# Attention scores in rounded parts and rests, each head on half of the array's rows

## The chip, the cores and the metric

The kernel runs on one core of one Trainium2 chip. The metric is the device time of that core in microseconds (us), from the kernel's start to its end. TensorE (PE) multiplies; its weight loads are listed apart as PEld. VectorE (DVE) and ScalarE (ACT) read what PE leaves in the PSUM banks, GpSimd (POOL) and SyncE (SP) issue transfers. The engines run each their own list in order and wait for one another on semaphores.

## What is computed

A recommendation tower over 1024 rows. Two encoders give, for every row, four "states" of 512 real and 512 imaginary numbers. Attention with 8 heads of 64 follows over the four states of a row; the change is in its scores:

```python
qr = heads(sr @ Wq_r.T + bq_r)
qi = heads(si @ Wq_i.T + bq_i)
kr = heads(sr @ Wk_r.T + bk_r)
ki = heads(si @ Wk_i.T + bk_i)
ar = einsum('bhnd,bhmd->bhnm', qr, kr) + einsum('bhnd,bhmd->bhnm', qi, ki)
ai = einsum('bhnd,bhmd->bhnm', qi, kr) - einsum('bhnd,bhmd->bhnm', qr, ki)
mag = sqrt(ar ** 2 + ai ** 2 + 1e-08) * HD ** (-0.5)
w = softmax(mag)
out_r, out_i = w @ vr, w @ vi          # then @ Wo_r.T + bo_r, @ Wo_i.T + bo_i
```

After it come a mixing of the states by their phases, two measurement matrices, and three layers that end in one number per row.

## The kernel before, in words

Most matrix products are made in three passes of 32-bit "rounded" numbers (`split3`, lines 53 to 55): each operand is held as a rounded part (hi) and the rest (lo), and hi·hi, hi·lo and lo·hi are added up in a PSUM bank.

The change lies in `phase_states`, in its first half. It runs over 16 blocks `b` of 64 rows (256 columns, since each row has four states; `C` = 256). In a block, `m` = 0 to 3 counts slices of 128 of the 512 features, so that each slice holds two heads `h` of 64. PE's order in a block (`block_body` of the tensor engine) is written out by hand and sets the order of the rest:

- `project(b, m, 0)` makes the queries of slice m in bank `b_q` (one buffer), real part in one half of the columns and imaginary in the other; `project(b, m, 1)` the keys in `b_k[:, m % 2]` (two buffers). Each is 24 products of 256 columns.
- from m = 1 on, after both: `t_turn(b-1, m-1)` turns the softmax weights `pd` of the block before (4 transposes), `score(b, m-1)` makes the scores, and `mix(b-1, m-1)` multiplies the turned weights with the values.
- after m = 3: `values(b, 0)` and `(b, 1)`, then the turn, score and mix of slice 3, then `values(b, 2)` and `(b, 3)`, then `project_out(b-1, m)` for all four slices.

Before the change the queries leave `b_q` on ACT (`q_evac`, four reads of 64 partitions by 256, line 1287) into `qs`, and the keys leave `b_k` on DVE (`k_evac`, eight reads of 64 by 256, line 1590) into `ks`. Both are laid out so that real and imaginary parts of one head stand one above the other on the 128 partitions. `score` (line 2004) then needs one plain 32-bit product per head and column group: four per slice, each of 128 rows of the array and 256 columns; the profile lists each as two instructions. For a head and a group, the product gives the real and the imaginary score at once, into bank `b_sc[:, h]`.

On ACT a slice then goes `q_evac(b, m)`, `pt_evac(b-1, m-1)` (the turned weights, line 1302), `t_square(b, m-1)` (both score banks squared, line 1296), `o_high(b-1, m-1)` (rounded part of the mixed output, line 1311). On DVE it goes `spread(b-1, m)` (the weights `pd`, one buffer, so it waits for `t_turn(b-1, m-1)`; line 1639), `k_evac(b, m)`, `o_low(b-1, m-1)` (the rests of the output, line 1648), `pick(b, m-1)` (sum, mask and reduction of the squares, lines 1600 to 1609). At the end of a block `t_high` and `t_low` (lines 1339 and 1659) split the projected outputs into the buffer `at` (`thi`, `tlo`), and SP stores them (`store_a`).

Of the kernel before, what the change touches and what calls it, by code (L numbers as in the profile page):

```python
# [906 lines left out]
def phase_states(nc, g):  # L907
# [15 lines left out]
    with s.ctx:  # L923
# [11 lines left out]
        qs = sb_t("qs", [P, 2, 2, C])  # L935
        ks = sb_t("ks", [P, 2, 2, 2, C])
# [7 lines left out]
        at = sb_t("at", [P, 2, 2, 2, C], F32R)  # L944
        thi, tlo = at[:, 0], at[:, 1]
# [51 lines left out]
        k_read = [s.sem(f"t_k_read{h}") for h in range(2)]  # L997
# [88 lines left out]
        K_PARTS = ((0, 0, 0, 1), (0, 1, 1, 1), (1, 0, 1, 1), (1, 1, 0, -1))  # L1086
# [169 lines left out]
        @block.gpsimd  # L1256
        def _(pool):
            def fold(t):
                pool.wait_ge(folded, t * 2 + 1)
                if not isinstance(t, int) or t < LAST:  # L1260
                    pool.wait_ge(newton, t * 2 + 3)
                pool.wait_ge(stored, t * 16)
                pool.tensor_tensor(sup[:, :, :], cs[:, :, 2, :], cs[:, :, 3, :], ALU.add).then_inc(folded, 1)

            pool.memset(k01[:, 0:1], FLOOR).then_inc(k_made, 1)
            pool.memset(k01[:, 1:2], 1.0).then_inc(k_made, 1)
            pool.wait_ge(ids_in, 16)
# [12 lines left out]
        def _(act):  # L1280
            def q_evac(b, m):
                if not isinstance(b, int) or 4 * b + m >= 2:
                    act.wait_ge(scored, b * 8 + (2 * m - 2))
                act.wait_ge(projected, b * 8 + (2 * m + 1))
                for e in range(2):
                    for h in range(2):
                        ins = act.activation(qs[half(e), m % 2, h, :], b_q[half(h), e * C:(e + 1) * C], ACT.Identity,
                                             bias=bcol(M_Q + e, m, half(h)))
                    ins.then_inc(q_read, 1)
# [57 lines left out]
            def block_body(b, first):  # L1347
                q_evac(b, 0)
                for m in range(1, KD):
# [24 lines left out]

            blocks(act, block_body)
# [207 lines left out]
        def _(dve):  # L1583
            def k_evac(b, m):
                if not isinstance(b, int) or 4 * b + m >= 2:
                    dve.wait_ge(scored, b * 8 + (2 * m - 2))
                dve.wait_ge(projected, b * 8 + (2 * m + 2))
                for h in range(2):
                    for e, part, at_half, sign in K_PARTS:
                        ins = dve.tensor_scalar(ks[half(at_half), m % 2, h, part, :], b_k[half(h), m % 2, e * C:(e + 1) * C],  # L1590
                                                bcol(M_K + e, m, half(h)), float(sign), ALU.add, ALU.mult)
                    ins.then_inc(k_read[h], 1)
# [78 lines left out]
            def block_body(b, first):  # L1671
                k_evac(b, 0)
# [281 lines left out]
        def _(pe):  # L1954
            def project(b, m, i):

                pe.wait_ge(w_split, (M_Q, M_K)[i] * KD + 2 * KD)
                if i == 0:
                    if not isinstance(b, int) or 4 * b + m >= 1:
                        pe.wait_ge(q_read, b * 8 + 2 * m)  # L1960
                elif not isinstance(b, int) or 4 * b + m >= 2:
                    for h in range(2):
                        pe.wait_ge(k_read[h], b * 4 + (m - 1))
# [12 lines left out]
            def values(b, i):  # L1976
                pe.wait_ge(w_split, M_O * KD)
                e, gr = i // 2, i % 2
                if i == 2:
                    pe.wait_ge(q_read, b * 8 + 8)  # L1980
                elif i == 3:
                    for h in range(2):
                        pe.wait_ge(k_read[h], b * 4 + 3)
# [10 lines left out]
            def score(b, m):  # L1994
                pe.wait_ge(q_read, b * 8 + (2 * m + 2))
                for h in range(2):
                    pe.wait_ge(k_read[h], b * 4 + (m + 1))
                for h in range(2):
                    if not isinstance(b, int) or 4 * b + m >= 1:
                        pe.wait_ge(t_squared, b * 8 + (2 * m - 1 + h))  # L2000
                    for gr in range(NG):
                        cols = slice(gr * P, (gr + 1) * P)
                        out = b_sc[:, h, :].rearrange("p (a g c) -> p a g c", a=2, g=NG)[:, :, gr]
                        mm = pe.matmul(out, qs[:, m % 2, h, cols], ks[:, m % 2, h, :, cols], start=True, stop=True)
                    mm.then_inc(scored, 1)
# [222 lines left out]
def build(nc, g):  # L2228
    with ExitStack() as ctx:
# [12 lines left out]
        g.k01 = s.sb("k01", [P, 2])  # L2242
        s.align(512)
# [104 lines left out]
```

## Time and profile before

| what | value |
|---|---|
| median of three runs | 2947.16 us (2946.24 to 2949.06) |
| the profiled execution's own time | 2950.54 us |
| its span, first to last instruction | 2948.7 us |
| mean granted TensorE clock | 0.979 of full speed |
| PE busy | 2815.6 us, 95% of the span |
| PEld, DVE, ACT busy | 2438.5, 2105.5, 1326.6 us |
| the stage with the change | from about 1428 to 2330 us |

Busy time is summed over instructions of one engine; a matmul's duration in the profile includes the time in which its last columns run through the array, while the next one has already begun, so the pace of PE is read from the starts of its instructions in the timeline and not from their mean durations. A timeline row is: start, length, engine, line, operation, out<-in, shape, number of merged instructions, and in brackets how long the engine was idle before it and what ended that.

### The profile page before, as it was taken

The numbers are of one execution on the slowest core, as the hardware profiler recorded it, in microseconds if no ns is written. First come the engines' busy times: TensorE is split into PE (matmuls) and PEld (weight loads), VectorE is DVE, ScalarE is ACT, GpSimd is POOL, SyncE is SP. The second block draws the span as 40 slices with busy tenths as digits, with TensorE's granted clock in tenths as the row PEclk, the third lists the DMA queues.
The fourth block names the chain that finished last, engine by engine and source line by source line (L and its number), as shares of the span: only waits on it lengthen the run. The fifth ranks groups of instructions, "written<-read, shape, count | busy, mean of one in ns | idle before, by whom it ended". The sixth has DMA issues, their size and how long they took to land. (4 is left out here: it accounts for less than half of the span.)

```text
span 2948.7 us, 40983 instructions
## 1 busy us (share of the span) xinstructions
PE 2815.6 (95%) x15040; PEld 2438.5 (83%) x15040; DVE 2105.5 (71%) x3170; ACT 1326.6 (45%) x2000; POOL 139.8 (5%) x177
## 2 busy tenths in 40 slices
PE   8999999998999989999699999999999899999797
PEld 6888888886788877888599999999999877777686
DVE  5788768763668856787667667766776759999863
ACT  2222432243534344333455555555555654555553
POOL 1000100001001010000001001000000000000000
PEclk9999999998999999999899999999999999999899
DMA  6565465545738776486422232233223464344310
GB/s 241 188 208 187 170 225 189 187 138 179 244 113 263 251 254 202 142 266 242 172 58 58 79 92 57 59 91 78 57 71 94 105 163 103 93 101 123 111 40 11
DMA packets 493712, 420.36 MB, mean 143 GB/s; under 512 B 282272, under 2 KB 397088, under 8 KB 493344
## 3 DMA queue, kind: packets, MB, share of 16 engines
q1 hardware_dynamic: 459168, 341.20, 38.2%
q0 software_dynamic: 17792, 60.89, 5.4%
q10 hardware_dynamic: 16640, 16.78, 1.7%
q8 instruction: 70, 1.15, 0.2%
q14 instruction: 42, 0.34, 0.0%
HBM read 328.62 MB, written 90.18 MB: 142 GB/s over the span
## 5 line engine op out<-in xcount | busy, mean ns | idle before, releaser
L53 PE MATMUL banks<-a_hi 128*128 128x512 f32 x1024 | 399.6, 390 | 14.3 <-DVE a_lo L353 14.3
L54 PE MATMUL banks<-a_lo,a_hi 128*128 128x512 f32 x1024 | 399.3, 390 | 0.0
L55 PE MATMUL banks<-a_hi,a_lo 128*128 128x512 f32 x1024 | 399.3, 390 | 0.0
L53 PE MATMUL banks<-b_hi 128*128 128x512 f32 x896 | 357.0, 398 | 24.3 <-DVE b_lo L760 14.0
L55 PE MATMUL banks<-b_hi,b_lo 128*128 128x512 f32 x896 | 352.5, 393 | 0.0
L54 PE MATMUL banks<-b_lo,b_hi 128*128 128x512 f32 x896 | 352.4, 393 | 0.0
L53 PE MATMUL banks<-t_sx,g_hi 128*128 128x256 f32 x1024 | 294.6, 288 | 26.5 <-DMA t_sx<-s_scr 26.5
L54 PE MATMUL banks<-t_sx,g_hi 128*128 128x256 f32 x1024 | 291.5, 285 | 0.0
L55 PE MATMUL banks<-t_sx,g_lo 128*128 128x256 f32 x1024 | 291.5, 285 | 0.0
L1590 DVE TENSOR_SCALAR t_ks<-banks,cols 64x256 f32<-64x256 f32 x512 | 236.5, 482 | 75.2 <-PE banks L55 67.9
L53 PEld LDWEIGHTS banks<-a_hi 128*128 128x128 f32 x1024 | 192.9, 188 | 54.6 <-DVE a_lo L353 14.7
L55 PEld LDWEIGHTS banks<-a_hi,a_lo 128*128 128x128 f32 x1024 | 192.8, 188 | 40.2
L54 PEld LDWEIGHTS banks<-a_lo,a_hi 128*128 128x128 f32 x1024 | 192.8, 188 | 40.0
L53 PEld LDWEIGHTS banks<-b_hi 128*128 128x128 f32 x896 | 170.4, 190 | 66.0 <-DVE b_lo L760 28.8
L53 PE MATMUL banks<-g_hi,s_axng 128*128 128x512 f32 x512 | 203.6, 398 | 18.2 <-DVE s_cs L1732 14.6
L53 PEld LDWEIGHTS banks<-t_sx,g_hi 128*128 128x128 f32 x1024 | 198.4, 194 | 27.2 <-issue 23.1
L54 PE MATMUL banks<-g_lo,s_axng 128*128 128x512 f32 x512 | 202.5, 395 | 0.0
L55 PE MATMUL banks<-g_hi,s_axng 128*128 128x512 f32 x512 | 202.3, 395 | 0.0
L55 PEld LDWEIGHTS banks<-b_hi,b_lo 128*128 128x128 f32 x896 | 170.4, 190 | 36.4
L54 PEld LDWEIGHTS banks<-b_lo,b_hi 128*128 128x128 f32 x896 | 170.8, 191 | 34.3
L54 PEld LDWEIGHTS banks<-t_sx,g_hi 128*128 128x128 f32 x1024 | 198.5, 194 | 0.1
L55 PEld LDWEIGHTS banks<-t_sx,g_lo 128*128 128x128 f32 x1024 | 198.3, 194 | 0.0
(192 smaller groups left out, 5828.9 us busy)
## 6 DMA issues: line engine op xcount, KB each, us to landing
w_ring<-w_first SPq DMA_DIRECT2D x192, 512.0 KB, 4.3
w_ring<-w_second SPq DMA_DIRECT2D x160, 512.0 KB, 5.0
t_sx<-s_scr SPq DMA_DIRECT2D x64, 512.0 KB, 4.3
a_scr<-t_at SPq DMA_DIRECT2D x256, 128.0 KB, 1.9
s_axng<-a_scr SPq DMA_DIRECT2D x64, 512.0 KB, 5.4
g_wraw<-w_pieces SPq DMA_DIRECT2D x74, 256.0 KB, 4.7
x_raw<-h_scr ACTq DMA_DIRECT2D x16, 1024.0 KB, 7.0
w_ring<-w_second SPq DMA_DIRECT2D x64, 256.0 KB, 5.0
```

Of the source, the lines that this page charges most:

```text
L53: mm(out, ahi, bhi, start=first, stop=False, **more)
L54: mm(out, ahi, blo, start=False, stop=False, **more)
L55: return mm(out, alo, bhi, start=False, stop=last, **more)
L1590: ins = dve.tensor_scalar(ks[half(at_half), m % 2, h, part, :], b_k[half(h), m % 2, e * C:(e + 1) * C], bcol(M_K + e, m, half(h)), float(s ...
```

## The change

The scores are made in three passes of rounded parts and rests instead of one plain 32-bit product, and each head works on its own half of the array's rows. Real and imaginary parts are no longer stacked on the partitions: each is a separate product that is added up in the bank. So a slice has 2 column groups x 2 (real, imaginary) x 3 passes x 2 heads = 24 products of 64 rows and 256 columns, and heads alternate: head 0 reads partitions 0 to 63 and writes bank `b_sc[:, 0]`, head 1 partitions 64 to 127 and bank `b_sc[:, 1]`.

For that, queries leave `b_q` as whole reads of 128 partitions: ACT writes the rounded part (two reads), DVE then the rest (`q_rest`, two). The keys move from DVE to ACT for the rounded part (`k_evac` there, three reads: imaginary, real, negated imaginary), and DVE writes the rest (`k_rest`, three). `b_q` is free for the next `project(b, m+1, 0)` only when `q_rest` is done. `qs` takes over the buffer `at`, so `q_evac` of slices 0 and 1 waits for the stores of block b-2, and `t_square` of the slice before is waited for in both heads before the first score. A column of negated biases `nbk` is made once on POOL.

```diff
@@ scalar
             def q_evac(b, m):
                 if not isinstance(b, int) or 4 * b + m >= 2:
                     act.wait_ge(scored, b * 8 + (2 * m - 2))
+                if m < 2 and (not isinstance(b, int) or b >= 2):
+                    act.wait_ge(a_stored[m], b * 128 - 64)
                 act.wait_ge(projected, b * 8 + (2 * m + 1))
                 for e in range(2):
-                    for h in range(2):
-                        ins = act.activation(qs[half(e), m % 2, h, :], b_q[half(h), e * C:(e + 1) * C], ACT.Identity,
-                                             bias=bcol(M_Q + e, m, half(h)))
-                    ins.then_inc(q_read, 1)
+                    ins = act.activation(qs[:, 0, m % 2, e, :], b_q[:, e * C:(e + 1) * C], ACT.Identity, bias=bcol(M_Q + e, m))
+                ins.then_inc(q_high, 1)
+
+            def k_evac(b, m):
+                act.wait_ge(projected, b * 8 + (2 * m + 2))
+                bank = b_k[:, m % 2, :]
+                act.activation(ks[:, 0, m % 2, 0, :], bank[:, C:2 * C], ACT.Identity, bias=bcol(M_K + 1, m))
+                act.activation(ks[:, 0, m % 2, 1, :], bank[:, 0:C], ACT.Identity, bias=bcol(M_K, m))
+                act.activation(ks[:, 0, m % 2, 2, :], bank[:, C:2 * C], ACT.Identity, scale=-1.0,
+                               bias=g.nbk[:, m:m + 1]).then_inc(k_high, 1)
...
                     if not first:
                         pt_evac(b - 1, m - 1)
+                    k_evac(b, m)
                     t_square(b, m - 1)
@@ vector
-            def k_evac(b, m):
...
+            def q_rest(b, m):
+                dve.wait_ge(q_high, b * 4 + (m + 1))
+                for e in range(2):
+                    ins = dve.scalar_tensor_tensor(out=qs[:, 1, m % 2, e, :], in0=b_q[:, e * C:(e + 1) * C],
+                                                   scalar=bcol(M_Q + e, m), in1=f32(qs[:, 0, m % 2, e, :]),
+                                                   op0=ALU.add, op1=ALU.subtract)
+                ins.then_inc(q_read, 1)
+
+            def k_rest(b, m):
+                dve.wait_ge(k_high, b * 4 + (m + 1))
+                bank = b_k[:, m % 2, :]
+                for part, e in ((0, 1), (1, 0), (2, 1)):
+                    ins = dve.scalar_tensor_tensor(out=ks[:, 1, m % 2, part, :], in0=bank[:, e * C:(e + 1) * C],
+                                                   scalar=bcol(M_K + e, m), in1=f32(ks[:, 0, m % 2, part % 2, :]),
+                                                   op0=ALU.add, op1=ALU.subtract, reverse1=part == 2)
+                ins.then_inc(k_read, 1)
...
                     if not first:
                         spread(b - 1, m)
-                    k_evac(b, m)
+                    q_rest(b, m)
+                    k_rest(b, m)
                     if not first:
                         o_low(b - 1, m - 1)
                     pick(b, m - 1)
@@ tensor
             def score(b, m):
...
+                q, k = qs[:, :, m % 2], ks[:, :, m % 2]
+                passes = [(e, x, y) for e in range(2) for x, y in ((0, 0), (0, 1), (1, 0))]
+                for gr in range(NG):
+                    cols = slice(gr * P, (gr + 1) * P)
+                    for i, (e, x, y) in enumerate(passes):
+                        for h in range(2):
+                            bank = b_sc[:, h, :].rearrange("p (a g c) -> p a g c", a=2, g=NG)[:, :, gr]
+                            mm = pe.matmul(bank, q[half(h), x, e, cols], k[half(h), y, 1 - e:3 - e, cols],
+                                           start=i == 0, stop=i == len(passes) - 1)
+                            if gr == NG - 1 and i == len(passes) - 1:
+                                mm.then_inc(scored, 1)
```

PE's list before, between the projections of slice 3 and the values (line 2014 is `t_turn`, 2004 `score`, 2025 `mix`; an `x4` stands for four products in a row):

```order
L55 MATMUL banks<-t_sx,g_lo 128x256
L2014 MATMUL banks<-ident,t_pd 128x128 x4
L2004 MATMUL banks<-t_ks,t_qs 128x2x128 x4
L2025 MATMUL banks<-t_ptl,t_v 128x128 x4
L53 MATMUL banks<-g_hi,t_sx 128x512
```

The same place after (`score` is line 2026 there):

```order
L55 MATMUL banks<-t_sx,g_lo 128x256
L2038 MATMUL banks<-ident,t_pd 128x128 x4
L2026 MATMUL banks<-t_ks,t_qs 128x2x128 x24
L2049 MATMUL banks<-t_ptl,t_v 128x128 x4
L53 MATMUL banks<-g_hi,t_sx 128x512
```

Nothing moves on PE; four products become 24.

DVE's list before, in the loop over the blocks, from slice 1's `spread` to that of slice 2 (`t_ks` is the keys' reads, `t_olo` the output's rests, `t_m` and `t_mg` the picking; the rows of registers belong to waits):

```order
L1639 SCALAR_TENSOR_TENSOR t_pd<-t_ex,t_inv,mask 128x128 x4
L1587 REGISTER_ALU
L1590 TENSOR_SCALAR t_ks<-banks,cols 64x256 x8
L1645 ISA
L1648 SCALAR_TENSOR_TENSOR t_olo<-banks,cols,t_ohi 64x256 x4
L1598 REGISTER_ALU
L1600 TENSOR_TENSOR t_m<-t_sq 128x512
L1604 REGISTER_ALU
L1605 TENSOR_TENSOR t_m<-t_m,mask 128x512
L1609 TENSOR_REDUCE t_mg<-t_m 128x16
L1637 REGISTER_ALU
L1639 SCALAR_TENSOR_TENSOR t_pd<-t_ex,t_inv,mask 128x128 x4
```

The same stretch after:

```order
L1659 SCALAR_TENSOR_TENSOR t_pd<-t_ex,t_inv,mask 128x128 x4
L1598 REGISTER_ALU
L1600 SCALAR_TENSOR_TENSOR t_qs<-banks,cols,t_qs 128x256 x2
L1609 SCALAR_TENSOR_TENSOR t_ks<-banks,cols,t_ks 128x256 x3
L1665 ISA
L1668 SCALAR_TENSOR_TENSOR t_olo<-banks,cols,t_ohi 64x256 x4
L1616 ISA
L1620 TENSOR_TENSOR t_m<-t_sq 128x512
L1625 TENSOR_TENSOR t_m<-t_m,mask 128x512
L1629 TENSOR_REDUCE t_mg<-t_m 128x16
L1657 REGISTER_ALU
L1659 SCALAR_TENSOR_TENSOR t_pd<-t_ex,t_inv,mask 128x128 x4
```

Eight reads become five, and the queries' rests now stand behind `spread`.

ACT's list before, the stretch of slice 2 in the loop:

```order
L1287 ACTIVATE t_qs<-banks,cols 64x256 x4
L1299 REGISTER_ALU
L1302 ACTIVATE t_ptl<-banks 128x512
L1295 REGISTER_ALU
L1296 ACTIVATE t_sq<-banks 128x512
L1293 REGISTER_ALU
L1296 ACTIVATE t_sq<-banks 128x512
L1311 ACTIVATE t_ohi<-banks,cols 64x256 x4
```

The same after:

```order
L1290 ACTIVATE t_qs<-banks,cols 128x256 x2
L1309 REGISTER_ALU
L1312 ACTIVATE t_ptl<-banks 128x512
L1294 REGISTER_ALU
L1296 ACTIVATE t_ks<-banks,cols 128x256
L1297 ACTIVATE t_ks<-banks,cols 128x256
L1298 ACTIVATE t_ks<-banks,g_nbk 128x256
L1305 REGISTER_ALU
L1306 ACTIVATE t_sq<-banks 128x512 x2
L1321 ACTIVATE t_ohi<-banks,cols 64x256 x4
```

The keys' three reads now stand between the turned weights and the squares.

## Rows read from the trace of the kernel before

**Rows 1.** The page: PE's busy time; granted clock in 40 slices of the span.

```profile
PE 2815.6 (95%) x15040; PEld 2438.5 (83%) x15040; DVE 2105.5 (71%) x3170; ACT 1326.6 (45%) x2000; POOL 139.8 (5%) x177
...
PEclk9999999998999999999899999999999999999899
```

**Rows 2.** Busy time by stretches; the attention stage.

```profile
core 0: us, PE busy (x) PEld busy (x) DVE busy (x) ACT busy (x) POOL busy (x), PEclk, DMA share, GB/s
...
1425.00:2330.00 905.00, 901.18 (x6435) 855.75 (x6435) 635.96 (x1485) 485.08 (x939) 30.85 (x32) 1.00 0.27 75
```

**Rows 3.** Groups by form, 1425 to 2330 us: busy, mean ns | idle before.

```profile
L1590 DVE TENSOR_SCALAR t_ks<-banks,cols 64x256 f32<-64x256 f32 x512 | 236.5, 482 | 75.2 <-PE banks L55 67.9
...
L2004 PE MATMUL banks<-t_ks,t_qs 128*128 128x256 f32 x512 | 121.2, 379 | 0.0
...
L1648 DVE SCALAR_TENSOR_TENSOR t_olo<-banks,cols,t_ohi 64x256 fp32r<-64x256 f32 x240 | 115.9, 483 | 6.5
...
L1339 ACT ACTIVATE t_at<-banks,cols 128x256 fp32r<-128x256 f32 x112 | 47.0, 471 | 79.2 <-DMA a_scr<-t_at 63.9 <-PE banks L55 15.2
```

**Rows 4.** Timeline of PE, slice 1 of a block, to the next turn.

```profile
1599.70 0.60 PE L2014 MATMUL banks<-ident,t_pd 128*128 128x128 f32 x4
1600.13 1.89 PE L2004 MATMUL banks<-t_ks,t_qs 128*128 128x256 f32 x8
1601.86 1.05 PE L2025 MATMUL banks<-t_ptl,t_v 128*128 128x128 f32 x8
1602.67 0.36 PE L53 MATMUL banks<-t_sx,g_hi 128*128 128x256 f32 x1
...
1604.91 0.28 PE L53 MATMUL banks<-t_sx,g_hi 128*128 128x256 f32 x1
1605.27 0.28 PE L53 MATMUL banks<-t_sx,g_hi 128*128 128x256 f32 x1
...
1608.51 0.60 PE L2014 MATMUL banks<-ident,t_pd 128*128 128x128 f32 x4
```

**Rows 5.** Timeline of DVE, the same stretch.

```profile
1600.34 1.14 DVE L1639 SCALAR_TENSOR_TENSOR t_pd<-t_ex,t_inv,mask 128x128 f32<-128x128 f32 x4 [2.41 <-PE banks L2014]
1601.51 3.79 DVE L1590 TENSOR_SCALAR t_ks<-banks,cols 64x256 f32<-64x256 f32 x8
1605.33 1.99 DVE L1648 SCALAR_TENSOR_TENSOR t_olo<-banks,cols,t_ohi 64x256 fp32r<-64x256 f32 x4
1607.35 0.69 DVE L1600 TENSOR_TENSOR t_m<-t_sq 128x512 f32<-128x512 f32 x1
...
1609.41 1.13 DVE L1639 SCALAR_TENSOR_TENSOR t_pd<-t_ex,t_inv,mask 128x128 f32<-128x128 f32 x4
```

**Rows 6.** Timeline of ACT, the same stretch.

```profile
1600.41 0.60 ACT L1302 ACTIVATE t_ptl<-banks 128x512 f32<-128x512 f32 x1 [1.46 <-PE banks L2014]
...
1602.06 0.60 ACT L1296 ACTIVATE t_sq<-banks 128x512 f32<-128x512 f32 x1 [0.18 <-PE banks L2004]
1602.96 1.93 ACT L1311 ACTIVATE t_ohi<-banks,cols 64x256 fp32r<-64x256 f32 x4 [0.29 <-PE banks L2025]
```

**Rows 7.** Weight loads of the turns: group over the stage, and one slice's timeline.

```profile
L2014 PEld LDWEIGHTS banks<-ident,t_pd 128*128 128x128 f32 x240 | 28.2, 140 | 2.0
...
1608.41 0.46 PEld L2014 LDWEIGHTS banks<-ident,t_pd 128*128 128x128 f32 x4
```

**Rows 8.** Timelines of DVE, ACT and PE at a block's end and the next's beginning.

```profile
1638.51 1.13 DVE L1659 SCALAR_TENSOR_TENSOR t_at<-banks,cols,t_at 128x128 fp32r<-128x128 f32 x4 [1.13 <-ACT t_at L1339]
...
1644.35 1.13 DVE L1659 SCALAR_TENSOR_TENSOR t_at<-banks,cols,t_at 128x128 fp32r<-128x128 f32 x4 [1.62 <-ACT t_at L1339]
...
1643.41 0.84 ACT L1339 ACTIVATE t_at<-banks,cols 128x256 fp32r<-128x256 f32 x2 [2.21 <-DMA a_scr<-t_at]
...
1649.00 1.93 ACT L1287 ACTIVATE t_qs<-banks,cols 64x256 f32<-64x256 f32 x4 [1.60 <-PE banks L55]
...
1648.80 0.28 PE L53 MATMUL banks<-t_sx,g_hi 128*128 128x256 f32 x1
```

More of the change, by code:

```diff
@@ L943, in phase_states @@
         olo = sb_t("olo", [P, KD, 2, C], F32R)
-        at = sb_t("at", [P, 2, 2, 2, C], F32R)
-        thi, tlo = at[:, 0], at[:, 1]
+        qs = sb_t("qs", [P, 2, 2, 2, C], F32R)
+        thi, tlo = qs[:, 0], qs[:, 1]
         mg2 = sb_t("mg2", [P, KD, GH, N])
@@ L996, in phase_states @@
         q_read = s.sem("t_q_read")
-        k_read = [s.sem(f"t_k_read{h}") for h in range(2)]
+        k_read = s.sem("t_k_read")
+        q_high = s.sem("t_q_high")
+        k_high = s.sem("t_k_high")
         v_full = s.sem("t_v_full")
@@ L1266, in _ @@
             pool.memset(k01[:, 1:2], 1.0).then_inc(k_made, 1)
+            pool.tensor_scalar(g.nbk[:, :], g.cols[:, COL_BC + (M_K + 1) * KD:COL_BC + (M_K + 2) * KD], -1.0, None,
+                               ALU.mult).then_inc(k_made, 1)
             pool.wait_ge(ids_in, 16)
@@ L1348, in block_body @@
                 q_evac(b, 0)
+                k_evac(b, 0)
                 for m in range(1, KD):
@@ L1373, in block_body @@
                         t_high(b - 1, m)
+            act.wait_ge(k_made, 3)
             blocks(act, block_body)
@@ L1583, in _ @@
         def _(dve):
-            def k_evac(b, m):
[L1585 to L1592, printed above, removed]
+            def q_rest(b, m):
[13 more added lines that the diff above has]
+                ins.then_inc(k_read, 1)
             def pick(b, m):
@@ L1671, in block_body @@
             def block_body(b, first):
-                k_evac(b, 0)
+                q_rest(b, 0)
+                k_rest(b, 0)
                 for m in range(1, KD):
@@ L1959, in project @@
                     if not isinstance(b, int) or 4 * b + m >= 1:
-                        pe.wait_ge(q_read, b * 8 + 2 * m)
+                        pe.wait_ge(q_read, b * 4 + m)
                 elif not isinstance(b, int) or 4 * b + m >= 2:
-                    for h in range(2):
-                        pe.wait_ge(k_read[h], b * 4 + (m - 1))
+                    pe.wait_ge(k_read, b * 4 + (m - 1))
                 if m == 0 and not (isinstance(b, int) and b == 0):
@@ L1979, in values @@
                 if i == 2:
-                    pe.wait_ge(q_read, b * 8 + 8)
+                    pe.wait_ge(q_read, b * 4 + 4)
                 elif i == 3:
-                    for h in range(2):
-                        pe.wait_ge(k_read[h], b * 4 + 3)
+                    pe.wait_ge(k_read, b * 4 + 3)
                 elif not isinstance(b, int) or b >= 2:
@@ L1994, in score @@
             def score(b, m):
[L1995 to L2005, printed above, removed]
+                pe.wait_ge(q_read, b * 4 + (m + 1))
+                pe.wait_ge(k_read, b * 4 + (m + 1))
+                if not isinstance(b, int) or 4 * b + m >= 1:
+                    pe.wait_ge(t_squared, b * 8 + 2 * m)
+                q, k = qs[:, :, m % 2], ks[:, :, m % 2]
[9 more added lines that the diff above has]
+                                mm.then_inc(scored, 1)
             def t_turn(b, m):
@@ L2242, in build @@
         g.k01 = s.sb("k01", [P, 2])
+        g.nbk = s.sb("nbk", [P, KD])
         s.align(512)
```

4 lines of the change are left out of this document (1 added, 3 removed).

## The prediction

> **What bounds the kernel now.** I read the page first: PE is busy for 95% of the span, at a granted clock of 0.8 to 1.0 [rows 1]. Then the busy times by stretches: in the stage that the change touches PE is busy for 901.2 of 905.0 us at full clock, DVE for 636.0 and ACT for 485.1 [rows 2]. So in this stage the time is PE's list of work, and a change is worth what it adds to or takes from that list, unless it makes PE wait. Then the timeline of one slice, counted from T, the start of its turn (1599.70): turn 0.43 us, score 1.73, mix 0.81, then two projections of 24 products each up to the next turn at T+8.81 [rows 4]. In the projections three products start every 0.36 us, so one every 0.12 us [rows 4]; nowhere does PE pause. DVE is a close second: its round of spreading, reading keys, output rests and picking takes from 1600.34 to 1609.41, 9.07 us, more than PE's 8.81 [rows 5]. It may fall behind for three slices since the keys have two banks and the time is made good while PE makes the values. ACT has room.
>
> **PE's part of the change.** Away go 8 instructions per slice, which take 1.73 us [rows 4]; their mean length of 379 ns [rows 3] holds the run through the array and isn't the pace. In come 24 products of 64 rows and 256 columns in rounded numbers. A product of that kind with 128 rows is paced at 0.12 us [rows 4]. The trace shows no product on half of the rows, so I bound the score time S from both sides:
> - heads fully side by side, 12 pairs by 0.12: S = 1.44 us. A still lower floor takes the spacing of the turns' weight loads, four in 0.46 us where one has 0.14, so (0.46 - 0.14) / 3 = 0.107, times 12: S = 1.28 [rows 7].
> - heads one after the other: 24 by 0.12, S = 2.88.
> - a price for going over to half arrays and back: a product is listed with 0.28 us but the next starts after 0.12 [rows 4], so 0.16 us of running through is hidden today. If PE has to run empty at both changes, that and one load of 0.11 are paid twice: 0.54 us per score. With pairs, S = 1.98; in series, S = 3.42.
>
> I take pairs, with half of the price of changing over: S = 1.44 + 0.27 = 1.71, nearly what it is today. The nearest fact in the rows is that loads and products of different instructions already go on together: PE and PEld are busy for 95% and 83% of the same span [rows 1]. The profile has nothing that speaks for or against the price, which is why I take its middle.
>
> What the Trainium skill says of it, in "TensorEngine Tiling (Array Packing)", Key Properties: different tiles of the array can load weights and multiply in parallel, but changing the tiling mode drains TensorE. By that page S would be 1.98 and the sum below about 9 us higher; no row of the trace shows either half of the rule.
>
> **The other engines' part.** DVE loses 8 reads of 482 ns and gains 5 of the kind that takes 483 [rows 3]: the rows' number of partitions doesn't count, their 256 elements do. That is 3.79 us against 5 x 0.483 = 2.42 per slice, 88 us less over 64 slices. ACT loses 4 reads of 0.48 (1.93 for the output's four of this shape, [rows 6]) and gains 5 of 0.471 (a 128x256 read, [rows 3]): 0.43 us more per slice. Neither is on the path by its sum. But the order matters, so I walk slice 1 of a block, in times from T:
>
> - ACT: turned weights at 0.71 to 1.31 [rows 6]. Then the keys' three rounded reads, 3 x 0.483 = 1.45: to 2.78 (they are projected before T). Then two squares of 0.60, which before started as soon as a bank was scored (the second at 2.36, [rows 6]) and now queue: to 4.02. Then the output's four rounded reads, 1.93: to 5.97 instead of 5.19 (1602.96 + 1.93).
> - DVE: spreading starts at 0.64 [rows 5], takes 1.17 with its gap, then the queries' rests 0.97 to 2.78, the keys' rests from 2.83 to 4.28. It then waits for ACT: 5.97 plus 0.10 (the step from ACT to DVE, 1643.41 + 0.84 to 1644.35, [rows 8]) = 6.07. Output rests 2.0 to 8.08, picking as before 2.06 until the next spreading can start (1607.35 to 1609.41, [rows 5]): 10.15.
> - Slice 2: DVE spreads 10.15 to 11.32, queries' rests to 12.28. Only now is `b_q` free. PE, which waits with `project(b, 3, 0)` behind mix, starts its first product after a step of 0.05 and a weight load of 0.11: T+12.43.
> - Before, that product came at one slice and the 2.97 us from turn to projection (1602.67 - 1599.70, [rows 4]): T+11.78. So the block loses 0.65 us here, whatever S is, as long as S stays below 2.0 or so: with S at 1.71, PE is there at T+8.79+2.95 = 11.74 and stands idle for 0.7.
>
> In slice 1 the rests are ready at T+2.83 and wanted at 0.43 + S + 0.81 = 2.95: nothing. In slice 3 no projection follows, and the picking of slice 2 ends in time. So per block with a block before it the sum is 0.65 + 2 x (S - 1.73), where the factor 2 is for the scores of slices 2 and 3, made after the wait; with S = 1.71 it is 0.61 us. Fifteen blocks: 9.2 us. Block 0 has no turn and no mix, and gets 4 x (S - 1.73) = -0.1. Sum +9.1 us.
>
> **What is hidden.** The queries share their buffer with outputs. The store of slice 0's output takes 3.77 us from the end of its split (1638.51 + 1.13) to the ACT read that it lets go (1643.41) [rows 8]. Slice 2's split ends at 1645.48, so its buffer is free at 1649.25; the queries' first read stood at 1649.00 [rows 8] and slips by 0.25. With 0.95 for it, 0.15 for two steps and 0.97 for the rests, `b_q` is free at 1651.32; PE wants it after the keys' 24 products, 1648.80 + 2.88 = 1651.68. The projection of the keys hides it, by 0.36 us; were a store later than that, it would cost what it is later, 14 times. SP and POOL get no new work in the loop; the negated bias column is one small POOL instruction. Waiting for both squares ahead of a score costs nothing: they end at 4.0, the next score starts at 9.2. The later last reads at the end of the stage lie beside the output projections.
>
> **Rivals.**
> 1. Weights are loaded in series though products run side by side. Then the 24 loads pace the score, 24 x 0.107 = 2.57 us [rows 7]: 0.84 more per slice, PE no longer waits for DVE, 64 x 0.84 = 53.8 us, 3001.0 us. For it: the turns' loads come 0.107 us apart although their products have half as many columns as the projections' [rows 7], as if the loads set that pace. Against it: loads of different halves read different partitions. The Trainium skill, "TensorE: Matmul & The Clock Gate", LDWEIGHTS, says that a load's time goes by its columns and not by its rows, so half of the rows saves nothing; it also says there, in Part 3, that a load overlaps running products only where the row groups differ, which the busy shares contradict: 95% and 83% of one span overlap, and all of it at 128 rows [rows 1].
> 2. The heads don't run side by side at all, the change doesn't do what it says: S = 2.88, 64 x 1.15 = +73.6, 3020.8 us; with the price of changing over, 64 x 1.69 = +108, 3055. For it: each row of PE in this trace has the form 128*128, so side-by-side work isn't seen once.
> 3. The other side, faster: pairs at 1.44, and PE never waits for `b_q`. That is decided on ACT: the output's rounded reads would have to end by about T+4.8 instead of 5.97, so that DVE spreads for slice 2 at T+9.0. Then each of the 64 scores gives 0.29 us: -18.6, 2928.6 us. For it: DVE has 88 us less work, and its order has slack that I may have walked too strictly. Against it: the same walk, made for the kernel before, gives 9.71 for DVE's next spreading, and it is at 1609.41 - 1599.70 = 9.71.
>
> **How the numbers follow.** The profiled execution took 2950.54 us, its span 2948.7; by the sum it would take 2959.6. The median of the runs lies 3.4 lower, at 2947.16, and the forecast goes by it: 2947.16 + 9.1 = 2956.3. The forecast's own range is that of S with pairs: S = 1.28 gives 15 x (0.65 - 0.90) - 1.8 = -5.6, 2941.6; S = 1.98 gives 15 x 1.15 + 1.0 = +18.3, 2965.4.
>
> Chances: forecast 0.50; rival 1, 0.19; rival 2, 0.19; rival 3, 0.12. The range 2938 to 3024 leaves out most of rival 3 and the costly end of rival 2. A measurement here can tell 0.2%, 5.9 us, from no change. Faster by more than that is rival 3 alone, 0.12. Within it lies the forecast with S below about 1.6, 0.22. Slower: the rest of the forecast, 0.28, and rivals 1 and 2, 0.66 in all.
>
> **What would show it.** In the timeline of PE after: the score of a slice, from its first product's start to the mix's, is S; two products of a pair start together if heads run side by side, and loads too. A wait of some 0.7 us ahead of the first projection of slice 3, ended by the queries' rests on DVE, and none ahead of slice 2's, shows the walk right; ACT's output reads should start near T+4.0. DVE's busy time should fall by 88 us, ACT's rise by some 27. The prediction is wrong if S is over 2.0, or if PE shows no wait, or if stores end later than the keys' projection hides.

## The result

The changed kernel takes 2955.06 us (median of 7 runs, 2951.81 to 2960.46), the kernel before 2947.74 (7 runs, 2946.17 to 2950.52). The ratio is 1.0026, with an interval from 1.0015 to 1.0038: 7.3 us slower. The forecast was 2956.3, slower by 9.1.

The page of the changed kernel, its busy times and granted clock:

```profile
PE 2824.7 (95%) x16064; PEld 2440.5 (82%) x16064; DVE 2003.2 (68%) x2978; ACT 1319.7 (45%) x2064; POOL 142.4 (5%) x178
...
PEclk9999999999999999999899999999999999999899
```

Against [rows 1] DVE has 102 us less and PE 9 more. ACT was forecast with 27 more and has 7 less.

The profiled execution's span is 2958.7 us, 10.0 more than before. Not all of that is the change. The same kernel, profiled again further below, has a span of 2949.2; the stretch from the last values of the stage to the end, which the change doesn't touch, takes 2958.7 - 2335.7 = 623.0 us in one and 2949.2 - 2333.2 = 616.0 in the other (622.1 before). So the stage itself must be compared: from its first product on PE, at 1424.3 us, to the last that the values begin with a `L53`, it takes 2335.7 - 1424.3 = 911.4 us (2333.2 - 1423.3 = 909.9 in the second profile) against 2326.6 - 1423.7 = 902.9 before. The change is worth 7.0 to 8.5 us there, as in the medians. These are the rows of the values' products, of the kernel before and then of the changed one. Each gives the shortest, median and longest duration in ns, and then the first and last start:

```profile
L53 PE MATMUL banks<-g_hi,t_sx x256: 389/389/580, 1454.3 to 2326.6; 128*128 128x512 f32 x128
```

```profile
L53 PE MATMUL banks<-g_hi,t_sx x256: 388/390/500, 1456.4 to 2335.7; 128*128 128x512 f32 x128
```

The same slice as in [rows 4 to 6], the first of its block that has a turn (slice 1 in the prediction's count), now on PE, weight loads, DVE and ACT (T = 1603.88 is the start of the turn):

```profile
1603.88 0.60 PE L2038 MATMUL banks<-ident,t_pd 128*128 128x128 f32 x4
1604.41 1.69 PE L2026 MATMUL banks<-t_ks,t_qs 64*128 64x256 f32 x24
1606.03 1.16 PE L2049 MATMUL banks<-t_ptl,t_v 128*128 128x128 f32 x8
1606.95 0.36 PE L53 MATMUL banks<-t_sx,g_hi 128*128 128x256 f32 x1
...
1612.78 0.60 PE L2038 MATMUL banks<-ident,t_pd 128*128 128x128 f32 x4
```

```profile
1604.41 1.49 PEld L2026 LDWEIGHTS banks<-t_ks,t_qs 64*128 64x128 f32 x24 [0.17 <-issue]
```

```profile
1604.52 1.14 DVE L1659 SCALAR_TENSOR_TENSOR t_pd<-t_ex,t_inv,mask 128x128 f32<-128x128 f32 x4 [3.69 <-PE banks L2038]
1605.58 0.87 DVE L1600 SCALAR_TENSOR_TENSOR t_qs<-banks,cols,t_qs 128x256 fp32r<-128x256 f32 x2
1606.36 1.26 DVE L1609 SCALAR_TENSOR_TENSOR t_ks<-banks,cols,t_ks 128x256 fp32r<-128x256 f32 x3
1609.19 1.99 DVE L1668 SCALAR_TENSOR_TENSOR t_olo<-banks,cols,t_ohi 64x256 fp32r<-64x256 f32 x4 [1.56 <-ACT t_ohi L1321]
```

```profile
1604.60 0.60 ACT L1312 ACTIVATE t_ptl<-banks 128x512 f32<-128x512 f32 x1 [2.55 <-PE banks L2038]
1605.09 0.47 ACT L1296 ACTIVATE t_ks<-banks,cols 128x256 fp32r<-128x256 f32 x1
1605.45 0.48 ACT L1297 ACTIVATE t_ks<-banks,cols 128x256 fp32r<-128x256 f32 x1
1605.80 0.48 ACT L1298 ACTIVATE t_ks<-banks,g_nbk 128x256 fp32r<-128x256 f32 x1
1606.22 1.09 ACT L1306 ACTIVATE t_sq<-banks 128x512 f32<-128x512 f32 x2
1607.23 1.92 ACT L1321 ACTIVATE t_ohi<-banks,cols 64x256 fp32r<-64x256 f32 x4
```

PE first. The array form now reads 64*128. The 24 products start within 1.69 - 0.28 = 1.41 us, 0.061 apart, 0.12 a pair: the heads do run side by side, and so do their loads, 24 in 1.49 us. But the score's own gain is eaten at its edges. From turn to score it is 0.53 us (before 0.43), from score to mix 1.62 (1.73), from mix to the first projection 0.92 (0.81): 3.07 in all instead of 2.97. A slice takes 8.90 us instead of 8.81.

On DVE and ACT: the keys' rounded reads are listed with 0.47 each but start 0.36 apart; three of DVE's end within 1.26 us. And PE doesn't wait for the rests outside block 0 and the last block. All of PE's waits in the stage that the waits view lists:

```profile
PE banks L53 <- DMA t_sx<-s_scr: 4.0, 1, 4.0
...
PE banks L53 <- DVE g_lo L1688: 1.4, 1, 1.4
...
PE banks L53 <- issue: 0.5, 1, 0.5
```

The first was 3.8 us before. The second is new and comes once, in block 0:

```profile
1445.79 1.69 PE L2026 MATMUL banks<-t_ks,t_qs 64*128 64x256 f32 x24
1448.92 0.36 PE L53 MATMUL banks<-t_sx,g_hi 128*128 128x256 f32 x1 [1.44 <-DVE g_lo L1688]
```

On DVE eight weight pieces (`g_lo`) stand ahead of the queries' rests that PE waits for; the view names the pieces, and the rests end at 1448.82:

```profile
1443.13 4.90 DVE L1688 TENSOR_TENSOR g_lo<-g_wraw,g_hi 128x512 fp32r<-128x512 f32 x8
1447.95 0.87 DVE L1600 SCALAR_TENSOR_TENSOR t_qs<-banks,cols,t_qs 128x256 fp32r<-128x256 f32 x2
```

One more wait is too short for that list. It is the wait of the prediction's walk, ahead of the first projection of slice 3, and it comes in the last block alone:

```profile
2312.32 0.88 DVE L1600 SCALAR_TENSOR_TENSOR t_qs<-banks,cols,t_qs 128x256 fp32r<-128x256 f32 x2
```

```profile
2313.29 0.36 PE L53 MATMUL banks<-t_sx,g_hi 128*128 128x256 f32 x1
```

The projection starts 0.09 us behind the end of the rests and 1.09 behind the first product of mix, instead of 0.92: PE loses 0.17 us, in both profiles of the kernel. DVE began its spreading there 1.09 us after the turn, and elsewhere 0.64 to 0.71 after it. In the other blocks the rests of this slice end 0.31 to 0.38 us before PE starts.

So the loss is made of: 14 blocks in which four slices take 0.31 us more (their turns follow at 8.90, 8.90, 8.61 and 31.64 us instead of 8.81, 8.82, 8.53 and 31.58), 4.3 us; the wait in block 0, 1.4 us; and the end of the loop and the last block with 1.2. Of these 1.2, 0.7 comes with the "issue" pause at 2295.3 us (listed with 0.49), for which nothing in the trace gives a cause. The second profile doesn't have it, so it isn't the change's own. That makes 6.9 us. In the profile with 8.5 us, 1.0 more lies behind the long wait for `t_sx` at 1474.9 us, where the granted clock over the next 12.7 us is 0.77, against 0.85 over 11.7 us before. It isn't the kernel's own either: in its second profile the clock there is again 0.85, and the first product behind that wait is listed with 0.38 us, as before (0.39), in this one with 0.58. The last 0.6 of the 8.5 us stay without an account. The second profile's 7.0 us hold something of their own too: a second wait for `t_sx` at 1427.3 us (1.17), by which its first score comes 0.4 us later. Some 6 to 7 us are left as the change's own.

### The profile page after: what moved, and what is told of

It is laid out like the page before. It is cut to its first block and busy times, and to the rows that moved or that the text cites. A ratio compares the mean times of both kernels' runs of the same rounds, so it can differ in the third digit from the quotient of the medians.

```text
span 2958.7 us, 42798 instructions
## 1 busy us (share of the span) xinstructions
PE 2824.7 (95%) x16064; PEld 2440.5 (82%) x16064; DVE 2003.2 (68%) x2978; ACT 1319.7 (45%) x2064; POOL 142.4 (5%) x178
## 5 line engine op out<-in xcount | busy, mean ns | idle before, releaser
L53 PE MATMUL banks<-a_hi 128*128 128x512 f32 x1024 | 400.4, 391 | 14.1 <-DVE a_lo L353 13.7
L53 PE MATMUL banks<-b_hi 128*128 128x512 f32 x896 | 357.5, 399 | 23.1 <-DVE b_lo L760 12.7
L53 PE MATMUL banks<-t_sx,g_hi 128*128 128x256 f32 x1024 | 295.6, 289 | 28.8 <-DMA t_sx<-s_scr 26.9
L53 PEld LDWEIGHTS banks<-a_hi 128*128 128x128 f32 x1024 | 193.0, 188 | 55.1 <-DVE a_lo L353 14.2
L53 PEld LDWEIGHTS banks<-b_hi 128*128 128x128 f32 x896 | 170.6, 190 | 65.6 <-DVE b_lo L760 28.4
L53 PEld LDWEIGHTS banks<-t_sx,g_hi 128*128 128x128 f32 x1024 | 199.0, 194 | 30.2 <-issue 24.0
L53 PE MATMUL banks<-g_hi,s_axng 128*128 128x512 f32 x512 | 204.7, 400 | 19.1 <-DVE s_cs L1754 15.8
L1668 DVE SCALAR_TENSOR_TENSOR t_olo<-banks,cols,t_ohi 64x256 fp32r<-64x256 f32 x256 | 123.6, 483 | 76.0 <-ACT t_ohi L1321 71.5
```

Of the source, the lines that this page charges most:

```text
L53: mm(out, ahi, bhi, start=first, stop=False, **more)
L1668: ins = dve.scalar_tensor_tensor(out=olo[half(h), m, e, :], in0=pm(b, m)[half(e), h * C:(h + 1) * C], scalar=bcol(M_V + e, m, half(h)), in ...
```

## The experiments

Two theories were put against each other. A: what the change loses is the price of going over to half arrays and back, about 0.4 us per slice, set against 0.3 gained by the three passes. B: the loss is that of the prediction's walk, PE held by the rests that DVE writes.

**Heads in turn.** Is it the alternation that pairs the heads?

```diff
-                for gr in range(NG):
-                    for i, (e, x, y) in enumerate(passes):
-                        for h in range(2):
+                for h in range(2):
+                    for gr in range(NG):
+                        for i, (e, x, y) in enumerate(passes):
```

> The changed kernel, but the 12 products of head 0 go ahead of the 12 of head 1 instead of alternating with them. In the changed kernel's trace a score's 24 products take 1.41 us from the first start to the last, 0.061 apart. Theory A (heads run side by side only where neighbours in the list use different halves): about 24 x 0.12 = 2.9 us per score, 1.4 us more for each of 64 scores, so about 2955 + 90 = 3045 us. Rival (the array looks ahead and pairs them anyway, or half-row products are simply paced at 0.06): no change, 2955 us.

Measured: 3022.5 us (2 runs), ratio 1.0241 (1.022 to 1.0261). PE's timeline of a slice:

```profile
1613.33 0.60 PE L2037 MATMUL banks<-ident,t_pd 128*128 128x128 f32 x4
1613.86 2.74 PE L2026 MATMUL banks<-t_ks,t_qs 64*128 64x256 f32 x24
1616.54 1.16 PE L2048 MATMUL banks<-t_ptl,t_v 128*128 128x128 f32 x8
```

The pairing goes. Score to mix is 2.68 us instead of 1.62, and 64 x 1.06 = 67.8 us is what the time rises by (3022.5 - 2955.1 = 67.4). The expectation of 90 had taken 0.12 per product; in series they start (2.74 - 0.28) / 23 = 0.107 apart, a little closer than whole-array products of as many columns. Products that stand 12 apart in the list are not paired.

**Whole rows.** The same number of columns without half arrays. The run leaves out the separation of the two heads.

```diff
-                            mm = pe.matmul(bank, q[half(h), x, e, cols], k[half(h), y, 1 - e:3 - e, cols],
-                                           start=i == 0, stop=i == len(passes) - 1)
+                        for x, y in ((0, 0), (0, 1), (1, 0)):
+                            mm = pe.matmul(bank, q[:, x, h, cols], k[:, y, 1 - h:3 - h, cols],
+                                           start=(x, y) == (0, 0), stop=(x, y) == (1, 0))
```

> The changed kernel, but each score is made of 12 products on all 128 rows (3 passes x 2 column groups x 2 banks) instead of 24 on 64 rows. It leaves out the separation of the heads: a bank gets the sum over both heads of the real or of the imaginary query with the keys. Reads on ACT and DVE are unchanged, and there are as many columns per score for the array as with perfect pairs. Theory A (what the change loses is the going over to half arrays and back, 0.10 + 0.21 + 0.11 = 0.42 us per slice by the trace of the changed kernel): turn to first projection 2.67 us instead of 3.07, 64 x 0.4 = 26 us less than the changed kernel, 2929 us, and 19 less than before. Theory B (the queries' rests on DVE hold PE, as the prediction's walk had it): PE would now wait for them, and the time stays near 2955 or falls only to 2945.

Measured: 2934.2 us, ratio 0.9944 (0.9927 to 0.9961). PE's and DVE's timeline of slice 2, whose rests the prediction had too late:

```profile
1605.54 0.60 PE L2037 MATMUL banks<-ident,t_pd 128*128 128x128 f32 x4
1605.89 1.68 PE L2026 MATMUL banks<-t_ks,t_qs 128*128 128x256 f32 x12
1607.40 1.06 PE L2048 MATMUL banks<-t_ptl,t_v 128*128 128x128 f32 x8
1608.39 0.39 PE L53 MATMUL banks<-t_sx,g_hi 128*128 128x256 f32 x1
```

```profile
1606.30 1.13 DVE L1659 SCALAR_TENSOR_TENSOR t_pd<-t_ex,t_inv,mask 128x128 f32<-128x128 f32 x4
1607.46 0.88 DVE L1600 SCALAR_TENSOR_TENSOR t_qs<-banks,cols,t_qs 128x256 fp32r<-128x256 f32 x2
```

Turn to score is 0.35, score to mix 1.51, and a mix without a wait, as in the other three slices, 0.81: 2.67 us, 0.40 less than with half arrays. That is the price of changing over. Of the 26 us only 21 arrive. In slice 2 mix to projection is 0.99 instead of 0.81, because the queries' rests end at 1608.34 and PE is there first. That is the wait of the prediction's walk, in the slice in which it was forecast and in no other: 0.18 us in each of 14 blocks and 0.56 in the last, 3.1 us. A wait of 1 us for the same rests at a block's beginning (1534.4 us) comes once. That leaves about 21. So both theories hold a piece here: A has the size, and B begins to bite as soon as PE's list is 0.4 us shorter.

**A fourth pass.** The price of a pair without the edges.

```diff
-                passes = [(e, x, y) for e in range(2) for x, y in ((0, 0), (0, 1), (1, 0))]
+                passes = [(e, x, y) for e in range(2) for x, y in ((0, 0), (0, 1), (1, 0), (1, 1))]
```

> The changed kernel with a fourth pass (rests times rests), 32 half-row products per score instead of 24, alternating as before. It measures the price of one more pair without that of changing over. Theory A (a pair costs 0.118 us, the rest of the score's 1.62 us to the mix is the price of changing back): 4 x 0.118 = 0.47 us more per score, 64 x 0.47 = 30 us more, 2985 us. Rival (each load of 64 rows is paid in series, 0.107 each, hidden so far elsewhere): 0.86 more per score, 3010 us.

Measured: 2985.5 us (2 runs), ratio 1.0115 (1.0095 to 1.0135), 30.4 us over the changed kernel.

```profile
1606.37 2.17 PE L2026 MATMUL banks<-t_ks,t_qs 64*128 64x256 f32 x32
1608.47 1.16 PE L2049 MATMUL banks<-t_ptl,t_v 128*128 128x128 f32 x8
```

Score to mix is 2.10 us, 0.48 more for four pairs: 0.12 a pair. The loads are not in series.

**Queries in halves.** Does the walk's wait come if the reads are slower?

```diff
-                    ins = act.activation(qs[:, 0, m % 2, e, :], b_q[:, e * C:(e + 1) * C], ACT.Identity, bias=bcol(M_Q + e, m))
+                    for h in range(2):
+                        ins = act.activation(qs[half(h), 0, m % 2, e, :], b_q[half(h), e * C:(e + 1) * C], ACT.Identity,
+                                             bias=bcol(M_Q + e, m, half(h)))
```

(and the same for the rests on DVE)

> The changed kernel, but the queries leave their bank in reads of 64 partitions, four on ACT and four on DVE instead of two and two, each from and to the same partitions. In the changed kernel's trace neighbouring reads of 128 partitions on one engine start 0.36 to 0.40 us apart though each is listed with 0.47, while the reads of 64 partitions of the output start 0.48 apart. Theory A (reads of half the partitions don't overlap their neighbours, whatever they cross): four take 1.9 us, the rests are done at the turn + 0.64 + 1.17 + 1.9 = 3.7 us, PE wants them at 3.07 and waits 0.7 in slices 1 and 2, and about 20 us are lost, 2975 us. Rival (only reads that cross from one half of the partitions to the other don't overlap): four take 1.55 us, ready at 3.4, wait 0.3, 2965 us. If the prediction's walk had the wrong order of dependence altogether: 2955 us.

Measured: 3007.5 us (2 runs), ratio 1.019 (1.0169 to 1.021), 52 us over the changed kernel. DVE, and PE's first projection behind it, at a block's beginning and in slice 1:

```profile
1602.73 1.98 DVE L1603 SCALAR_TENSOR_TENSOR t_qs<-banks,cols,t_qs 64x256 fp32r<-64x256 f32 x4 [2.71 <-ACT t_qs L1291]
...
1612.31 1.98 DVE L1603 SCALAR_TENSOR_TENSOR t_qs<-banks,cols,t_qs 64x256 fp32r<-64x256 f32 x4
```

```profile
1604.76 0.39 PE L53 MATMUL banks<-t_sx,g_hi 128*128 128x256 f32 x1 [1.51 <-DVE t_qs L1603]
...
1614.35 0.38 PE L53 MATMUL banks<-t_sx,g_hi 128*128 128x256 f32 x1 [0.42 <-DVE t_qs L1603]
...
1624.04 0.39 PE L53 MATMUL banks<-t_sx,g_hi 128*128 128x256 f32 x1 [0.54 <-DVE t_qs L1603]
```

Four reads of half the partitions take 1.98 us on DVE though nothing crosses from one half to the other, so it isn't a crossing within a read that keeps such reads from overlapping. Nor is it that they are half as high, as the expectation had it. The eight key reads of the kernel before have 64 partitions too, and their single starts follow at 0.49, 0.40, 0.48, 0.51, 0.50, 0.41 and 0.50 us, the same in all 64 slices. The third and the seventh, which start 0.40 and 0.41 after their neighbour, are the two whose bank half and target half are those of the read before; at each of the other five steps one of the two halves changes. In this run every read uses the other half than its neighbour, and no step is under 0.48. So on DVE it is the change of half between neighbours that costs 0.1 us a read. No run has these reads sorted by halves.

The waits of the walk are there, 0.42 and 0.54 listed. None of the expectations had the largest: 1.51 us at the block's beginning. There ACT's queries wait for the store of the shared buffer, read for 1.91 us, and DVE for 1.98; the 0.36 us of cover that the prediction gave to the shared buffer are gone. PE's waits ahead of these projections are, in all,

```profile
PE banks L53 <- DVE t_qs L1603: 32.2, 39, 2.0
...
PE banks L53 <- issue: 9.5, 8, 2.5
```

The waits called "issue" stand at the same projections, in blocks 0, 1 and the last. By the listed length of a product (0.28 us) and the pace of 0.12, a wait is listed only from 0.16 us after the next product could have begun; with that, 47 waits make 32.2 + 9.5 + 7.5 = 49 us. The wait in block 0, 1.6 us of it when counted so, was there already, which leaves 47.6 of the 52 us.

**The changed kernel again, and the pieces of block 0.** Is the pause in block 0 the wait of the one bank `b_q` for DVE? The changed kernel was measured again for comparison.

> The changed kernel once more, unaltered, beside the kernel before and beside the next two on one chip. Both theories: 2955 us, 0.26% over before, since nothing differs; it is the measure for the next two.

Measured: 2956.6 us (8 runs), the kernel before 2949.5 (18 runs), ratio 1.0024 (1.0014 to 1.0035).

```diff
-                    if first and m == 1:
-                        pieces(M_V * KD, M_O * KD)
+                    if first and m < 3:
+                        pieces(M_V * KD + (m - 1) * KD, M_V * KD + m * KD)
```

(on ACT and DVE)

> The changed kernel, but in block 0 the 8 weight pieces that ACT and DVE split after slice 1 are shared out, 4 after slice 1 and 4 after slice 2. In the changed kernel's trace PE is idle once in block 0 for 1.44 us, ended by such a piece on DVE, since the queries' rests of slice 2 stand behind the 8 pieces. Theory A (that pause is the single bank b_q waiting for DVE): it goes, and with it 1.4 us, 2953.6 us. Rival (the values, which need all 8 pieces, wait instead for as long): no change, and a pause ahead of the values in place of the old one.

Measured: 2953.1 us (11 runs), ratio 1.0013 (1.0004 to 1.0022). Of PE's waits for DVE the list then has only this one, at 2338.9 us, which the kernel before has with the same 0.5:

```profile
PE banks L53 <- DVE t_qs L1679: 0.5, 1, 0.5
```

The pause of 1.44 us is gone, and no other took its place. The medians of the two kernels differ by 3.5 us, more than that; the intervals of their ratios overlap, so the trace's 1.4 is the better number.

**Turns in between.** The price of changing over, paid twice.

```diff
-                    if not first:
-                        t_turn(b - 1, m - 1)
-                    score(b, m - 1)
+                    if first:
+                        score(b, m - 1)
+                    else:
+                        score(b, m - 1, range(0, 1))
+                        t_turn(b - 1, m - 1)
+                        score(b, m - 1, range(1, NG))
```

> The changed kernel, but the four turns of a slice stand between the two column groups of the score (12 half-row products, turns, 12 half-row products) instead of ahead of it. Same instructions, but PE goes over to half arrays and back twice per slice instead of once, in the 60 slices that have a turn. Theory A (going over and back costs about 0.4 us each time, as the run with whole rows showed: turn to score 0.35 us against 0.53, and so on): 60 x 0.4 = 24 us more than the changed kernel, 2979 us. Rival (the 0.4 us are no price of changing but of something else that comes once per score, such as the wait on semaphores or the last product's way through the array): no more than 60 x 0.1 = 6 us, 2961 us.

Measured: 2987.4 us, ratio 1.0121 (1.0106 to 1.0137), 30.8 us over the changed kernel's 2956.6 measured beside it. This is slice 1 of a block:

```profile
1608.15 0.98 PE L2027 MATMUL banks<-t_ks,t_qs 64*128 64x256 f32 x12
1609.06 0.66 PE L2039 MATMUL banks<-ident,t_pd 128*128 128x128 f32 x4
1609.65 0.98 PE L2027 MATMUL banks<-t_ks,t_qs 64*128 64x256 f32 x12
1610.56 1.15 PE L2050 MATMUL banks<-t_ptl,t_v 128*128 128x128 f32 x8
1611.73 0.39 PE L53 MATMUL banks<-t_sx,g_hi 128*128 128x256 f32 x1
```

In slice 3, behind which no projection waits for queries, the distance between turns grows from 8.61 to 8.94 us: a second going over and back costs 0.33 us, somewhat less than the 0.40 of the first. Four times per block that is 1.3 us, 20 us in all. The other 11 come from slices 1 and 2, whose turns follow at 9.52 and 9.65 us instead of 8.90: mix to projection is 1.17 and 1.31 instead of 0.92, since with the turns 0.9 us later spreading and the queries' rests are late again. The rival's 6 us is out.

**Whole rows with the rests on POOL.** Can the gain of three whole-row passes be had? This version makes three passes on whole rows, without half arrays: real and imaginary parts stacked as in the kernel before, rounded on ACT out of SBUF, the rests subtracted on POOL, which had been nearly idle. Its core:

```diff
+                    pool.wait_ge(highs, b * 12 + 3 * m + 1)
+                    pool.tensor_tensor(tlo[:, m % 2, :, :], qraw[:, m % 2, :, :], f32(thi[:, m % 2, :, :]), ALU.subtract).then_inc(lows, 1)
...
-                        mm = pe.matmul(out, qs[:, m % 2, h, cols], ks[:, m % 2, h, :, cols], start=True, stop=True)
+                        mm = split3(pe.matmul, out, thi[:, m % 2, h, cols], tlo[:, m % 2, h, cols],
+                                    khi[:, m % 2, h, :, cols], klo[:, m % 2, h, :, cols], True, True)
```

> A version that uses what the runs showed. The kernel before, with the scores in three passes of rounded parts and rests as in the change, but on all 128 rows with real and imaginary parts stacked as before (12 products, no going over to half arrays). The reads out of the banks stay as before (64 partitions, raw); ACT then rounds queries and keys from SBUF in whole reads (one of 128x512 and two of 128x512 per slice, 0.6 us each), and POOL, idle until now, subtracts for the rests (three of 128x512, about 1.2 us each by its 2.375 us for 128x1024). The embedding gathers of POOL are shared out over the slices. Theory A (the half arrays' price is what ate the gain, and three passes on whole rows cost 1.51 us after a turn of 0.35 against 1.73 and 0.43): 0.30 us less per slice than before, 64 x 0.30 = 19 us, 2929 us. Rival: the chain DVE read, ACT rounding, POOL rest is late for the next score (walked: keys' second head ready at the turn + 8.2 us, wanted at 9.6, and DVE's round of 9.07 us is now longer than PE's 8.5), or POOL and DVE slow each other: PE waits 0.3 us or more per slice, and the time is that of before, 2948 us, or more.

Measured: 2966.6 us, ratio 1.0059 (1.0046 to 1.0073), as the rival had it. PE's waits in the stage, two of its rows, and DVE's and POOL's timelines:

```profile
PEld banks L2037 <- DVE t_olo L1673: 25.2, 28, 1.4
...
PE banks L2037 <- DVE t_olo L1673: 19.8, 31, 1.0
```

```profile
1727.06 3.79 DVE L1615 TENSOR_SCALAR t_kraw<-banks,cols 64x256 f32<-64x256 f32 x8
1730.87 2.00 DVE L1673 SCALAR_TENSOR_TENSOR t_olo<-banks,cols,t_ohi 64x256 fp32r<-64x256 f32 x4
1732.90 1.55 DVE L1625 TENSOR_TENSOR t_m<-t_sq 128x512 f32<-128x512 f32 x1
...
1743.21 0.69 DVE L1625 TENSOR_TENSOR t_m<-t_sq 128x512 f32<-128x512 f32 x1
```

```profile
1731.36 2.55 POOL L1286 TENSOR_TENSOR t_klo<-t_kraw,t_khi 128x512 fp32r<-128x512 f32 x2 [2.10 <-ACT t_khi L1312]
```

The turns wait for the output's rests on DVE, whose round (9.07 us before the change, [rows 5]) is longer than the 8.5 us that PE would need. And the rounds get longer beside POOL. The sum of squares takes 0.69 us in the 51 slices in which a POOL subtraction lies beside it for less than 0.1 us, and 1.0 to 1.6 in the 13 in which it is more. With spreading, and the masking that follows the sum, DVE has 28 us more in the stage than in the kernel before. How much of PE's waits each of the two makes isn't shown, since no run has DVE's long list without POOL. In 12 slices PE also waits for the turned weights on ACT, 0.2 us listed. What this version keeps, and the change had got rid of, are DVE's eight half reads. None of these runs beats the kernel before with the right scores: the one that is faster leaves out the separation of the heads.

## Why the prediction was right, and where it wasn't

Time, sign and range held. But the sum was right by errors that cancel: the forecast 9.1 us come from a wait that isn't there, and the measured 7 from a price that was put too low and a wait that wasn't foreseen. That is luck, and the steps deserve each its own verdict.

- **Heads side by side: right.** 0.12 us a pair, as taken from the projections' pace; alternation is what makes them pair. Rivals 1 and 2 (loads or products in series) are out: 24 loads start within 1.49 us, and a pair more costs 0.12.
- **The price of changing over: mis-sized.** The prediction took half of 0.54, 0.27 us. It is 0.40 by the run with whole rows, 0.33 for a second one. It also lies on both sides of the score, 0.10 before it and 0.11 behind the mix, so S by itself, 1.62, looked better than the forecast 1.71, and the stretch from turn to projection, 3.07, worse than the forecast 2.95. Of the bounds, the upper one, running empty at both changes, was the nearer. The Trainium skill's sentence that a change of tiling mode drains TensorE ("TensorEngine Tiling (Array Packing)", Key Properties) agrees with the 0.40 us that are lost here. That the array runs empty is not seen in these traces; they show the price alone.
- **PE waits for the queries' rests in slice 2, 0.65 us a block: wrong.** It waits in the last block alone, 0.17 us. The step that failed is "3 x 0.483 = 1.45" for the keys' reads on ACT, and with it the 0.97 for two and the 1.20 for two squares. Whole-partition reads overlap their neighbours: three take 1.13 us from the first to the next instruction, two squares 1.01, and ACT's output reads start at T+3.35 instead of 4.04. DVE then starts the output's rests at T+5.31 instead of 6.07, with shorter reads before them, and is ready for slice 2's spreading when PE is. The row that said so was in the prediction's own list: two reads of 128x256 within 0.84 us [rows 8]. The pace was taken from the reads of 64 partitions, the only ones in the slice, and with it the sentence that a read's number of partitions doesn't count. It counts here through the halves: reads of half the partitions that change the half from one to the next start 0.48 to 0.51 us apart. The order of the wait was right: it shows with 0.2 us in slice 2 when the score is shorter, and with 0.4 to 0.5 when the queries' reads don't overlap. The cover that keeps it away in the changed kernel is only 0.3 to 0.4 us.
- **Block 0: missed.** The prediction counted -0.1 us there. The single bank `b_q`, now freed by DVE, stood behind eight weight pieces, 1.44 us. The diff showed the order; block 0 wasn't walked.
- **Shared buffer hidden: right**, with little cover, as the run with reads in halves shows.
- **Busy times: DVE -88 forecast, -102 measured; ACT +27 forecast, -7 measured.** Both for the overlap of whole reads.
- **Rival 3 (faster)** was right that PE doesn't wait for `b_q`, but not by its condition: ACT's output reads end at T+5.27, not by T+4.8, and DVE spreads for slice 2 at T+9.54, not T+9.0. It is enough because the turn itself comes at T+8.90 and the rests behind the spreading take 0.88 us. And it had priced the score at a perfect 1.44 with no change over: 64 x 0.40 = 26 us of price against its 18.6 of gain leave 7 us of loss, the measured time.

Forecast terms: 15 x 0.65 = 9.8 from the wait, -0.6 and -0.1 from the score. Measured terms in the trace: 4.3 from the edges of the score, 1.4 from block 0, and 1.2 from the end of the loop and the last block (0.5 without the pause that only one profile has).

## What to carry to other kernels

Products of half the array's rows run side by side if neighbours in PE's list use different halves (and here different banks; no run tries one bank for both), and then cost half each; but count what going over and back costs at the edges (0.40 us here, against 0.30 that three whole-row passes gain over the plain product). Group as many of them as possible between two changes, and spend them only where the gain per group is larger. When reads of a bank are costed, take the distance between starts of the very form that the change will use, not the listed length and not the pace of a neighbouring form. On DVE it may pay to sort reads of half the partitions so that neighbours stay on one half: by the starts of the key reads that saves 0.1 us a read, but no run tried it. And where a buffer gets a new owner that frees it, walk the first pass of the loop by itself: what stands ahead of that owner there may be something that the steady state never has.

## What the runs showed of the hardware that was not expected

- ACT and DVE start a read of 128 partitions by 256 about 0.36 to 0.40 us after the one before, though each is listed with 0.47 to 0.48. On DVE a read of 64 partitions by 256 starts as soon, 0.40 to 0.41 after its neighbour, if both read from the same half and write to the same half; if one of these halves changes, it starts 0.48 to 0.51 after it. It makes no difference whether a single read crosses from one half to the other (1.98 us for four that don't, 1.99 for four that do). Splitting a read by partitions costs more than twice when the halves take turns: 1.98 us for four against 0.88 for two. On ACT all half reads change a half and start 0.47 to 0.50 apart; none that stays on one half is in these runs.
- Half-row products in series start 0.107 us apart, whole-row products of the same columns 0.12.
- A subtraction on POOL of 128x512 takes 1.26 to 1.32 us, and 1.5 to 2.1 in 14 of 192 cases. DVE's SBUF-to-SBUF sum of the same size goes from 0.69 to as much as 1.6 us beside it (13 of 64; the other 51 have less than 0.1 us of a subtraction beside them and keep 0.69); DVE's reads of PSUM banks (3.79 us for eight) and its reduction (0.69) stay as they are.
